# Four-layer NHWC kernel on one Trainium2 core: the two scan layers on a centred residual, with transposes in place of centring matmuls and the whole convolution on VectorE

## What is computed

```
def scan_layer(x):                                   # x: 4 x 32 x 32 x 96
    h = layernorm(x, n1_g, n1_b) @ w_in + b_in       # 96 -> 192 channels
    h = depthwise_conv3x3(h, k_conv)                 # 9 taps a channel
    rows = ema(h, along=W) + ema(h, along=W, reverse=True)
    columns = ema(h, along=H) + ema(h, along=H, reverse=True)
    h = h + 0.25 * (rows + columns)                  # as the kernel folds it: fixed 128x128 matrices
    x = x + layernorm(h, on_g, on_b) @ w_out + b_out # 192 -> 96
    return x + gelu(layernorm(x, n2_g, n2_b) @ w1 + b1) @ w2 + b2   # hidden 384
# ema: y[t] = 0.6 * y[t-1] + 0.4 * h[t]
```

## Time and profile of the kernel before

| | |
|---|---|
| median of three executions | 3876.5 us (3875.81 to 3879.96) |
| profiled execution, its own time | 3877.88 us |
| its span in the trace | 3876.2 us |
| TensorE / its weight loads busy | 3407.6 us (88%) / 2480.4 us (64%) |
| VectorE / ScalarE / GpSimd busy | 2561.0 us (66%) / 1763.7 us (46%) / 504.7 us (13%) |
| preparation of the scan layers | 3225.24 to 3231.8 us of the span |
| the scan layers | 3233.0 us to the end, 3876.2 us: 643.2 us |

### The profile page before, as it was taken

The page is one execution under the profiler, slowest core; times in us unless marked ns, Lnnn a source line. Parts: engine busy times, 40 slices in busy tenths (PEclk is TensorE's granted clock), DMA queues, the critical chain, the costliest instruction groups (busy, mean ns, idle before and its releaser), DMA issues. The chain is left out here.

```text
span 3876.2 us, 140997 instructions
## 1 busy us (share of the span) xinstructions
PE 3407.6 (88%) x51142; PEld 2480.4 (64%) x51142; DVE 2561.0 (66%) x12038; ACT 1763.7 (46%) x5428; POOL 504.7 (13%) x2308
## 2 busy tenths in 40 slices
PE   5388999999769479999999999999999978999998
PEld 1145565666424148888888888888888864656655
DVE  4578999999757347777777777777777773333321
ACT  2117999999721154444444444444444442322232
POOL 0001000010000002222222222222222210000000
PEclk9689999999979775555555555555555557889898
DMA  1403333333210000000000000000000000000000
GB/s 31 131 16 108 115 104 105 102 109 121 74 50 0 16 2 5 5 4 5 5 5 5 5 5 5 5 5 5 5 5 5 5 4 10 1 1 1 1 9 9
DMA packets 54627, 116.33 MB, mean 30 GB/s; under 512 B 12313, under 2 KB 19801, under 8 KB 53692
## 3 DMA queue, kind: packets, MB, share of 16 engines
q1 hardware_dynamic: 37104, 53.42, 5.0%
q0 software_dynamic: 13824, 50.34, 3.7%
q10 hardware_dynamic: 2956, 3.15, 0.4%
HBM read 84.06 MB, written 22.81 MB: 28 GB/s over the span
## 5 line engine op out<-in xcount | busy, mean ns | idle before, releaser
L504 PE MATMUL g_zr<-g_hp,g_wp 97*128 97x4 f16 x24576 | 1088.3, 171 | 66.7 <-issue 48.4
L504 PEld LDWEIGHTS g_zr<-g_hp,g_wp 97*128 97x128 f16 x24576 | 956.8, 108 | 230.8 <-DVE g_hp L555 163.9
L597 ACT ACTIVATE g_e<-g_tn 96x8 f32<-96x8 f32 x2048 | 438.1, 214 | 694.6 <-DVE g_tn L541 694.6
L480 PE MATMUL g_zr<-s_inner,g_wi 96*128 (+2 forms) x6240 | 585.4, 234 | 58.9 <-issue 36.7
L555 DVE TENSOR_TENSOR_SCAN g_hp<-g_gates,g_e 96x16 f16<-96x16 f32 x2048 | 383.5, 187 | 343.4 <-ACT g_e L597 237.3
L614 POOL COPY s_y<-g_hs 96x8 f32 x2048 | 406.3, 198 | 1442.6 <-DVE g_hs L557 1442.6
L594 ACT ACTIVATE g_gates<-g_zr 96x16 f32<-96x16 f32 x2048 | 399.4, 195 | 312.5 <-PE g_zr L504 312.5
L511 PE MATMUL g_n<-g_hp,g_wp 97*128 97x8 f16 x8192 | 520.1, 174 | 0.0
L846 DVE CUSTOM_DVE_ANT_0 a_negated<-a_scores,a_mask 128x1024 f32<-128x1024 f32 x384 | 468.3, 1220 | 57.0 <-PE a_scores L764 40.9
L872 ACT ACTIVATE a_probs<-a_negated,a_negmax 128x1024 f32<-128x1024 f32 x384 | 442.4, 1152 | 25.4 <-DVE a_negmax L846 15.7
L541 DVE TENSOR_TENSOR_SCAN g_tn<-g_gates,g_n 96x24 f32<-96x24 f32 x2048 | 386.3, 189 | 95.9 <-ACT g_gates L594 91.1
(11 more groups left out here) (295 smaller groups left out, 3222.2 us busy)
## 6 DMA issues: line engine op xcount, KB each, us to landing
a_mask<-in_L_mask POOLq DMA_DIRECT2D x96, 512.0 KB, 5.9
a_k<-k_rows SPq DMA_DIRECT2D x96, 144.0 KB
q_rows<-r_q_parts SPq DMA_DIRECT2D x12, 576.0 KB, 7.3
k_rows<-r_k_parts SPq DMA_DIRECT2D x12, 576.0 KB, 7.4
a_q<-q_rows SPq DMA_DIRECT2D x96, 72.0 KB
o_parts<-a_o_sb SPq DMA_DIRECT2D x384, 18.0 KB
o_part<-o_parts SPq DMA_DIRECT2D x32, 192.0 KB
out_x<-x SPq DMA_DIRECT2D x4, 384.0 KB, 3.0
```

The lines of the kernel that those rows point to most:

```text
L480: pe.matmul(o, wi[0:K, half, pw, d * NG + g, :], x, start=first, stop=False, skip_group_check=True)
L504: mm = pe.matmul(zr_bank[u, k][:, 1 - g, d, :, at], wp[0:97, part, (2 * u + d) * NG + g, :], hp[u][0:97, d * NB:(d + 1) * NB, e], start=False,
L597: act.activation(e1[u][:, :, 0], tn[u][:, :, 2], ACT.Tanh, scale=to_tanh).then_inc(n_ok[u], 1)
```

## The change

- The residual is kept centred over the channels in a new tensor `res` of 97 rows, the mean as row 96. An item of L2 is centred once (a 96x97 matrix, which gives the mean too) and copied into `res`; L3 takes it from there. w_out, w2 and their biases are centred in the preparation and get a 97th column, the mean. A new stage g restores `x` from `res` for the four images of L3 (L2's need none) one slot after stage m, so there are 12 slots. ScalarE copies that out and SP stores it.
- The centring product of stage m, and of stage f for L3, is gone; so are two ScalarE copies.
- Tiles are turned by TensorE transposes of 96x128 tiles (four for each pair, 32 an item) instead of 96x192 products. ScalarE takes each pair with two instructions that also sum over the channels (`accum_out`), and VectorE centres the tokens in two instructions of 128x1536 an item (`centre_tokens`).
- The norm factors: variance weights become 128 columns wide, so each factor lies four times on the partitions; root and reciprocal are 128x128. GpSimd splits each reciprocal into three bf16 parts (`split`, four dependent instructions), and `spread_half` multiplies by 128-row bf16 weights, one pass.
- For stage e GpSimd adds the two halves of the squares (96x1024), so that 8 variance products do where there were 16. Its variance now stands before the down projection, and the rest of the norm, w_out and the adding stand at the start of the next slot.
- `convolve` is gone: VectorE does all nine taps on both 96-channel halves.
- The queue orders of all engines are rewritten; `ema_prepare` gains the column sums, subtractions, larger constants, and loses the diagonal matrices.

```diff
-            def convolve(v):
...
-                    mm = pe.matmul(turn[0][0:C, :], weights(v)["diag"][:, tap, :],
...
+            def split(parts, inv, inverted, i, done):
+
+                po.wait_ge(inverted, i + 1)
+                po.tensor_copy(parts[:, :], inv[:, :]).then_inc(done, 1)
+                po.wait_ge(done, 4 * i + 1)
+                po.tensor_tensor(inv[64:128, :], inv[64:128, :], parts[64:128, :], ALU.subtract).then_inc(done, 1)
+                po.wait_ge(done, 4 * i + 2)
+                po.tensor_copy(parts[64:128, :], inv[64:128, :]).then_inc(done, 1)
+                po.wait_ge(done, 4 * i + 3)
+                po.tensor_tensor(parts[96:128, :], inv[96:128, :], parts[96:128, :], ALU.subtract).then_inc(done, 1)
...
-                            mm = pe.matmul(turn[p % 2][:, s * 2 * C:(s + 1) * 2 * C], block_of, centre192[:, m, :],
-                                           start=(s == 0 and m == 0), stop=(m == 1), skip_group_check=True)
+                            at = (2 * s + m) * C
+                            mm = pe.transpose(turn[p % 2][:, at:at + C], tile, ident[0:C, 0:C])
...
             for k in slots:
-                f, v, e, m = stages(k)
...
+                f, v, e, m, g = stages(k)
+                if f is not None and f < NB:
...
+                        pe.matmul(mix[0][0:R, bank(h)], centre[:, :], x[:, part(f, h)], start=True,
+                                  stop=True).then_inc(f_centred, 1)
+                if k >= 3 and m is not None:
+                    pe.wait_ge(e_rooted, m + 1)
                 if e is not None:
                     pe.wait_ge(tapped, 2 * TAPS * (e + 1))
+                    turn_pairs(e, range(0, 2))
+                if k >= 4 and m is not None:
+                    pe.wait_ge(m_added, 2 * (k - 3))
...
+                if m is not None:
+                    pe.wait_ge(e_split, 4 * (m + 1))
+                    for h in range(2):
+                        spread_half(ring[h], h, e_parts, e_spread)
...
+                            mm = pe.matmul(ring[h][0:R, :], weights(m)["w_out"][:, s, :], e_xn[:, s, bank(h)],
+                                           start=(s == 0), stop=(s == 1))
+                        mm.then_inc(out_ready, 1)
+                if g is not None:
...
+                        pe.matmul(ring[h][0:C, :], uncentre[:, :], res[:, part(g, h)], start=True,
+                                  stop=True).then_inc(whole, 1)
                 if f is not None:
                     pe.wait_ge(f_squared, f + 1)
+                    if g is not None:
+                        pe.wait_ge(unloaded, 2 * (g - NB + 1))
+                    elif m is not None:
+                        pe.wait_ge(e_added, 2 * (m + 1))
+                    variance(ring[0], collect[C], f_squares, f_var)
                 if e is not None:
+                    turn_pairs(e, range(2, 6))
                 if f is not None:
+                    pe.wait_ge(f_split, 4 * (f + 1))
                     for h in range(2):
+                        spread_half(ring[h], h, f_parts, f_spread)
                     project_in(f, 0)
                 if e is not None:
+                    turn_pairs(e, range(6, 8))
                 if f is not None:
                     project_in(f, 1)
                 if m is not None:
+                    pe.wait_ge(m_squared, m + 1)
...
+                    variance(ring[0], collect[C], m_squares, m_var)
+                if e is not None:
...
+                    pe.wait_ge(token_centred, 2 * (e + 1))
+                    mix_tile(0)
+                if m is not None:
+                    pe.wait_ge(m_split, 4 * (m + 1))
+                    for h in range(2):
+                        spread_half(ring[h], h, m_parts, m_spread)
                     project_up(m, range(0, 2))
                 if e is not None:
                     mix_tile(1)
                 if m is not None:
+                    project_up(m, range(2, 6))
+                if e is not None:
+                    pe.wait_ge(e_summed, e + 1)
+                    variance(turn[1], collect[2 * C], e_squares[:, 0, :], e_var)
                 if m is not None:
                     for h in range(2):
+                        pe.wait_ge(gelu_ok, 2 * FT * m + 5 + h)
...
                         mm.then_inc(down_ready, 1)
```

More of the change, by code:

```diff
@@ L1345, in _ @@
             act.wait_ge(set_up, 1)
-            for w in layers:
-                for tap in range(TAPS):
-                    act.activation(w["diag"][:, tap, :], ident[0:C, 0:C], ACT.Identity, scale=w["taps"][:, 1, tap:tap + 1])
+            act.wait_ge(filled, 7)
+            for part in PARTS:
+                rows = slice(part, part + 32)
+                act.activation(chosen[rows, :], ident[rows, part:part + TURNS], ACT.Copy).then_inc(chosen_ok, 1)
+            act.wait_ge(chosen_ok, len(PARTS))
+            act.activation(spread[:, :, :], chosen[:, :].unsqueeze(2).broadcast_to([128, TURNS, 128]), ACT.Copy)
         @block.tensor
@@ L1647, in _ @@
+                if e is not None:
+                    take_turns(e, range(0, 2))
+                if g is not None:
+                    for h in range(2):
+                        act.wait_ge(whole, 2 * (g - NB) + h + 1)
+                        act.activation(x[:, part(g, h)], ring[h][0:C, :], ACT.Copy).then_inc(unloaded, 1)
                 if f is not None:
                     root(f_dev, ring[0], f_var, f + 1, f_rooted)
+                if e is not None:
+                    take_turns(e, range(2, 4))
@@ L1699, in invert, with centre_tokens, add_back @@
                 ve.reciprocal(to[:, :], dev[:, :]).then_inc(done, 1)
+            def centre_tokens(e, way):
+                ve.wait_ge(turn_taken, TURNS * e + 4 * (way + 1))
+                blocks = slice(TURNS * way, TURNS * (way + 1))
+                total = sums[:, blocks].unsqueeze(2).broadcast_to([128, TURNS, 2 * C])
+                ve.scalar_tensor_tensor(tokens[:, blocks, :], total, -0.5 / C, tokens[:, blocks, :], ALU.mult,
+                                        ALU.add).then_inc(token_centred, 1)
+            def add_back(ready, i, column, added):
+                for h in range(2):
+                    ve.wait_ge(ready, 2 * i + h + 1)
+                    ve.scalar_tensor_tensor(res[:, part(i, h)], ring[h][0:R, :], weights(i)["bias"][:, column:column + 1],
+                                            res[:, part(i, h)], ALU.add, ALU.add).then_inc(added, 1)
             for k in slots:
-                f, v, e, m = stages(k)
+                f, v, e, m, g = stages(k)
+                if m is not None:
+                    invert(e_inv, e_dev, e_rooted, m + 1, e_inverted)
                 if v is not None:
@@ L1712, in _ @@
                 if v is not None:
[L1713 to L1719 removed]
+                    taps(v, 5, 6)
                 if m is not None:
+                    if m:
+                        ve.wait_ge(up_ready, 2 * FT * m)
```

406 lines of the change are left out of this document (208 added, 198 removed).

## The result

The changed kernel takes 3746.96 us (median of three, 3744.6 to 3747.31) against 3876.5: ratio 0.9662, 95% interval 0.964 to 0.9684. The gain is 129.5 us; the forecast said 151, the range 3693 to 3795. The span is 3745.3 us.

What follows compares the result with a forecast made beforehand. TensorE bounded each slot, busy 72.7 of 78.4 us; afterwards the chain would, at 53.9. Slots and store summed to 3719.2, preparation made the span 3725.5, 3727.2 profiled, forecast 3726 us; forecast band 3710 to 3750, range 3693 to 3795.

Steps and rivals of the forecast that it cites:

- The mechanism: Full slot: TensorE stops being the bound; the chain through the engines sets 53.9 us where 78.4 stood.
- One sign of being wrong: List of what would show the forecast wrong: GpSimd's instructions over 0.8 us.
- Start to w_out's addition: First stretch of a full slot's chain: reciprocal, split, spreading, products, w_out at 1.2 GHz, addition; 11.9 us.
- From there to the first tile: Second stretch of the chain: variance and split of f, w_in, variance m; from 11.9 to 28.9 us.
- From the first tile to the last addition: Last stretch of the chain: two mixing tiles, w1, GELU, variance e, w2, addition; 25.0 us.
- the price of a split: GpSimd's split of a reciprocal into bf16 parts: 1.5 us with four hand-overs, bounds 1.0 and 2.5.
- the rival on GpSimd: GpSimd sets the pace: 0.6 to 1 us more an instruction beside taps, 3770 to 3800; chance 0.1.
- The 28 us that TensorE was to lose: TensorE's busy time per full slot: diagonal products, turning, centring, spreadings and variance products save some 28 of 72.7 us.
- the sum of 3725.5: Forecast span of the whole kernel: slots and store to 3719.2, plus 6.3 us later preparation.
- Low clock nearly throughout: Rival on TensorE's clock: sparse turning and split waits keep 1.2 GHz, 17 us a full slot, 3860; chance 0.1.
- Full clock under w_in: Rival: transposes and a 1.5 us wait don't lower the clock, 3.2 us a slot less, 3703; chance 0.12.
- Slower, and bound by VectorE: Two rivals: GpSimd instructions at 2.6 us give 3917, chance 0.03; bound moves to VectorE, no gain, chance 0.01.

Runs made afterwards that it cites:

- dense turning: Changed kernel with tiles turned by the old 192-column centring products, 64 records an item, without ScalarE's sums and `centre_tokens`: 3751.06 us, ratio 0.9668.
- three reliefs of TensorE: Changed kernel with half the convolution back on TensorE, 192-column turning and fp32 spreading, all three undone together: 3807.91 us, ratio 0.9817.

## Why the prediction was right, and where its sizes were off

- **The mechanism held.** TensorE no longer bounds a slot: 44.5 us busy (38 to 45 forecast), VectorE 34.4 (35), and the chain through the engines sets 56 us. The steps of the chain that I listed are in the timeline in the order given, except that the split of f ends 1.1 us behind tap 2, where I had it end first. The time, 3746.96 us, is 21 us over the forecast and inside its 3710 to 3750 by 3 us.
- **One sign of being wrong came true.** I had listed GpSimd's instructions over 0.8 us, and four of them in slot 6 took 1.18 to 1.28. It did show a wrong price; it did not show a wrong mechanism, since the extra time is 2.2 us of a 56.1 us slot.
- **The chain, piece by piece, in slot 6.** Start to w_out's addition 13.4 us (3489.51 to 3502.89) against 11.9: the split of e 2.35 instead of 1.5, w_out 7.14 instead of 6.9, the rest spreading at the low clock (1.01). From there to the first tile 17.7 against 17.0: the split of f 3.4 instead of 1.5, half of it paid back by an error of the sum the other way, since from the start of w_in's first half to that of its second 4.6 us passed and not the 5.7 of the sum: the last eight transposes ran while ScalarE was still copying the first half. From the first tile to the last addition 25.05 against 25.0: the split of m, as slow as that of f, was hidden behind the tile but for 0.5 us.
- **The term that was mis-sized** is the price of a split: "with four hand-overs 1.5 us a split, bounds 1.0 and 2.5". It measured 3.4 us for f and m and 2.35 for e. Alone, the instructions cost what I took them to (0.29, 0.42, 0.29, 0.42, and hand-overs). The upper bound failed because it was made from GpSimd's own rows, none of which had a tap beside it; the sentence "Tap 0 lies beside the split" names the neighbour and prices it at nothing. Yet the rival on GpSimd had it: 0.6 to 1 us more an instruction beside taps that read two tensors. Its size holds for the first two instructions (0.9 us more each), not for the others, which found no tap beside them: 1.9 us for each of two splits and 0.9 for the third. The sum of 96x1024 took 2.36 us, against 2.3.
- **The spreading.** The 28 us that TensorE was to lose count 4.5 us for three spreadings, while the sentence on them also says 3 at most. They gave 4.8, near the 4.5 by luck: in slot 6 they took 1.01, 1.03 and 0.62 us, two of the three at the low clock and not 0.5, but the one of m had stood at the low clock before, at 3.50 us and not the 1.98 of the other two.
- **The balance.** The span is 19.8 us over the sum of 3725.5. Slots 4 to 7 give 9.4 of it (225.0 against 215.6), slots 8, 9 and 10 2.3, 0.8 and 1.7; slot 3 is as forecast, and the tail 0.4 shorter. The remaining 6.2 lie ahead of slot 3: the preparation was 1.3 us cheaper than my 6.3, but slots 0 to 2, where I counted the clock as full, ran into the low one: the first half tile took 3.62 us and the variance of e 3.78, against 1.91 and 1.95 later, and in slots 1 and 2 the split of f took 3.4 us. (In slot 0, with no tap beside it, it had its 1.65.)
- **The rivals.** Low clock nearly throughout: no, 0.85 in slot 6. Full clock under w_in: no in the change; with dense turning, yes. GpSimd sets the pace: in part, as told. Slower, and bound by VectorE: no.
- **Transposes** cost 0.11 us each at the full clock, as I had it. That undoing them would cost nothing beyond the noise I did not see. I had counted their saving as TensorE's time, which was no longer the limit, and had weighed the rule of the Trainium skill (TensorE: Matmul & The Clock Gate, Part 4: PE-mode transpose) as a cost over the whole slot (3860) and not as one on the next product.

## What to carry to other kernels

When a part of the work goes off the bounding engine the question is what the chain needs next: here three reliefs of TensorE were worth 61 us together and 8 us counted one by one, since the kernel can do without any one of them before TensorE is the limit again. A short helper on GpSimd is priced with what VectorE runs beside it, and put where VectorE waits. And a large product right behind a wait is worth looking at for its clock: filling the wait before w_out with work that nobody needs was worth 22.5 us, and turning dense instead of sparse, 9 us of TensorE's time more in a slot, cost next to nothing. Look at several slots before believing what one shows of the clock.

## What was not expected of the hardware

- A GpSimd instruction of 0.29 or 0.43 us that met a tap on VectorE ended 0.15 to 0.29 us behind the tap and so took up to 1.28 us, and a one-input tap held it just as the others did.
- Ten records of unread products in a 3.5 us wait halved the time of w_out's 8 records behind it (7.14 to 3.67 us), with the granted clock at 1.00 instead of 0.50.
- The same rows of TensorE at the same distances over 11 us were followed by w_in's four records in 1.96, 3.22 or 3.73 us.
- 64 products of 96 columns an item kept the clock no better than 32 transposes; 64 of 192 columns did.
- A ScalarE copy with a sum is followed by an instruction of its own that reads the accumulator, 0.19 to 0.23 us, overlapped so that such a pair starts every 0.30 us: in a full slot TensorE waited for them 0.5 us at most at a time, in slots 8 and 9 up to 0.9.
